# Turning all eight blocks of the gathered rows by DMA instead of four by DMA and four by TensorE

## The chip, the cores and the metric

The kernel runs on one core of a Trainium2 chip. The metric is the device time of one execution in microseconds (us); the time of a kernel is the median of its runs.

## The reference, cut to what matters

Four sequences of 512 tokens with 512 channels go through a gated attention-like layer and then a mixture-of-experts layer. The second one is where the change lies (2048 tokens, 8 experts with 352 hidden channels, two experts for each token):

```python
def _L0_ffn_ref(x, gate_w, gate_bias, shared_gw, shared_dw, up_w, down_w):
    xf = x.reshape(-1, C)
    yg = xf @ shared_gw.T
    y, g = jnp.split(yg, 2, axis=-1)
    shared = jax.nn.silu(g) * y @ shared_dw.T
    scores = jax.nn.sigmoid(xf @ gate_w.T)
    _, topk_idx = jax.lax.top_k(scores + gate_bias, 2)
    w = jnp.take_along_axis(scores, topk_idx, axis=-1)
    w = w / jnp.sum(w, axis=-1, keepdims=True)
    out = jnp.zeros_like(xf)
    for e in range(8):
        we = jnp.sum(jnp.where(topk_idx == e, w, 0.0), axis=-1)
        g_e, u_e = jnp.split(xf @ up_w[e].T, 2, axis=-1)
        out = out + (jax.nn.silu(g_e) * u_e) @ down_w[e].T * we[:, None]
    return (shared + out).reshape(B, T, C)
...
x = x + jnp.tanh(g_ffn[0]) * _L0_ffn_ref(_layernorm(x, axis=-1), ...)
```

## The kernel before, in words

**Before the experts.** The first 300 us hold the attention part, the shared expert and the router, batch by batch. The normalised rows of all tokens go to a table in HBM, `xn_rows`, in which each row is stored twice: 512 float16 numbers that are the rounded value (the high part), and 512 more that are what the rounding lost (the low part). The shared expert's result is stored to the output before the experts add to it.

**The expert tiles.** The router sorts the 4096 pairs of token and expert by expert into tiles of 128 rows, each tile of one expert; with the padding there are 39 (`SLOT_TILES`). For tile t:

- GpSimd gathers the tile's 128 rows, high and low part, 1024 columns, from `xn_rows` into one of four buffers (`gather`, line 562; `GATHERS` is 4). This is an indirect DMA, as are the adds below, and both go over one software queue.
- The rows must be turned so that the channels lie on the partitions, in blocks of 128 x 128: four blocks of the high part, four of the low. This is done in two ways. For tiles 0 to 7 (`BY_DMA` is 8) TensorE transposes all eight blocks into a bank of PSUM (`turn_gathered`, line 1053, and `turn_rows`, line 881, whose matmuls are on line 883), and VectorE copies them into the operand buffer `x_t` (`gathered_turned`, line 1608). For tiles 8 to 38 TensorE transposes the four high blocks alone and VectorE copies these; the four low blocks are turned by a DMA transpose that SyncE issues (`turn_low`, line 424) into one of four buffers `x_low`, two of which are halves of `x_t`.
- TensorE multiplies with the expert's up weights (`up`, line 1088; the matmuls of lines 1101 and 1102), ScalarE and VectorE form the hidden values, TensorE transposes them (line 1111) and multiplies with the down weights (`down`, line 1114; line 1121).
- ScalarE scales the result by the router's weight into one of two buffers `rows` (`expert_rows`, line 813; the activation is on line 816).
- GpSimd adds these 128 rows into the output in HBM by an indirect DMA that accumulates (`add_rows`, line 567; line 569). Two tiles can hold rows for the same token.

**What sets the order.** Everything is written out by hand, each engine its own list, with semaphores between them. TensorE's list in the expert tiles (`expert_steps`, line 1140) is: down of tile t, transposes of the gathered rows of tile t+3, the first half of up of tile t+2, the hidden transposes of tile t+1, the second half of up of tile t+2. From tile 8 on this is a loop of four tiles a turn; the tiles' experts are read from a table at its start. GpSimd's list is: gather tile t+4, wait until the add of tile t-1 has landed, add tile t:

```python
for t in range(SLOT_TILES):
    if t + GATHERS < SLOT_TILES:
        after(pool, xt_mm, TILES + t + 1)
        if t >= BY_DMA:
            after(pool, xl_ld[t % GATHERS], (t - BY_DMA) // GATHERS * 16 + 16)
        gather(t + GATHERS)
    if t:
        rows_added(t - 1)
    add_rows(t)
```

So a gather waits until the buffer's last tile has been turned, by TensorE (`xt_mm`) and by DMA (`xl_ld`). `rows_added` waits for the landing of an add and only then frees its buffer in `rows` (`rows_free`); ScalarE waits for that before it writes the buffer again, and TensorE's next down matmuls wait until ScalarE has emptied their bank (`y_sb`). SyncE's list in these tiles holds the DMA transposes alone, in the order of the tiles; each waits for its gather (`g_ld`) and for the up matmuls that last read its buffer (`up_mm`). The up matmuls wait for VectorE's copy (`xt_sb`) and, from tile 8 on, for the DMA transpose (`xl_ld`).

Of the kernel before, what the change touches and what calls it, by code (L numbers as in the profile page):

```python
# [3 lines left out]
BATCHES, SEQ, C, D = 4, 512, 512, 128  # L4
# [66 lines left out]
def build(nc, x, ctx_t, wq, wk, gates, gate_wt, gate_bias, weights, out, xn_rows):  # L71
# [12 lines left out]
    with ExitStack() as ctx:  # L84
# [44 lines left out]
        def work_buf(words):  # L129
            used[0] += words  # L130
            return work[:, used[0] - words:used[0]]
# [7 lines left out]
        x_low_more = work_buf(C).bitcast(F16).rearrange("p (s a c) -> p s a c", s=2, a=KC)  # L139
# [4 lines left out]
        x_low = [x_t[:, n, KC:, :] for n in range(2)] + [x_low_more[:, n, :, :] for n in range(2)]  # L144
# [27 lines left out]
        lg = sb("lg", [P, TILES, 2, EXPERTS])  # L172
        r = [m.rearrange("p (t e) -> p t e", t=TILES) for m in (wq_s, wk_s)]
        r += [sb(f"r{n}", [P, TILES, EXPERTS], F16 if n == 2 else F32) for n in range(2, 6)]
# [155 lines left out]
        def _(sp):  # L330
# [93 lines left out]
            def turn_low(t):  # L424
                after(sp, g_ld[t % GATHERS], (t // GATHERS + 1) * 16)
                after(sp, up_mm, Q0 + t - (2 if t < BY_DMA + 2 else GATHERS) + 1)
                sp.dma_start_transpose(out=x_low[t % GATHERS], in_=xg_slots[t % GATHERS][:, C:2 * C]).then_inc(xl_ld[t % GATHERS], 16)

            for t in range(BY_DMA, SLOT_TILES):
                turn_low(t)  # L430
# [4 lines left out]
        def _(pool):  # L435
# [149 lines left out]
            for t in range(SLOT_TILES):  # L585
                if t + GATHERS < SLOT_TILES:
                    after(pool, xt_mm, TILES + t + 1)
                    if t >= BY_DMA:
                        after(pool, xl_ld[t % GATHERS], (t - BY_DMA) // GATHERS * 16 + 16)
                    gather(t + GATHERS)  # L590
                if t:
                    rows_added(t - 1)
                add_rows(t)
# [246 lines left out]
        def _(pe):  # L840
# [40 lines left out]
            def turn_rows(src, bank_, blocks=2 * KC):  # L881
                for n in range(blocks):
                    mm = pe.transpose(bank_[:, n, :], src[:, n * P:(n + 1) * P], ident16[:])  # L883
                mm.then_inc(xt_mm, 1)
# [168 lines left out]
            def turn_gathered(t, slot, n, bank_=xt_ps, blocks=2 * KC):  # L1053
                pe.wait_ge(g_ld[slot], (n + 1) * 16)
                if bank_ is xt_ps:
                    after(pe, xt_sb, ROWS_DVE + t)
                turn_rows(xg_slots[slot], bank_, blocks)
# [30 lines left out]
            def up(t, p, item, ks, low=None, low_n=None):  # L1088

                if 0 in ks:  # L1090
                    after(pe, hid_sb, Q0 + t - 1)
                    after(pe, xt_sb, ROWS_DVE + t + 1)
                    if low is not None:
                        after(pe, xl_ld[low], low_n * 16)
                for k in ks:
                    at = k * 2 * H
                    for part in range(2):
                        lhs = x_low[p if low is None else low][:, k, :] if part else x_t[:, p, k, :]
                        for half in range(2 - part):
                            begin, end = (k, part, half) == (0, 0, 0), (k, part) == (KC - 1, 1)  # L1100
                            pe.matmul(pg[p][:, 0:H], lhs, w[:, item, half, at:at + H], start=begin, stop=end)  # L1101
                            mm = pe.matmul(pu[p][:, 0:H], lhs, w[:, item, half, at + H:at + 2 * H], start=begin, stop=end)  # L1102
                if KC - 1 in ks:
                    mm.then_inc(up_mm, 1)
# [23 lines left out]
            def turn_and_up(t, p, item, low=None, low_n=None):  # L1128
                up(t, p, ds(item, 1), range(0, KC // 2), low, low_n)
                turn_hidden(t - 1, 1 - p)  # L1130
                up(t, p, ds(item, 1), range(KC // 2, KC), low, low_n)
# [8 lines left out]
            def expert_steps(t0, n0, steps, turn=True, late=False, dma_from=0):  # L1140
                down_item = item_of(t0)
                for k in range(steps):
# [5 lines left out]
                    if turn:  # L1148
                        turn_gathered(t0 + k + 3, (k + 3) % GATHERS, n0 + (k + 3) // GATHERS,
                                      blocks=KC if k + 3 >= dma_from else 2 * KC)  # L1150
# [13 lines left out]
            expert_steps(t, t // GATHERS, 1, turn=False)  # L1164
# [7 lines left out]
        def _(dve):  # L1172
# [435 lines left out]
            def gathered_turned(t, p, uses, bank_=xt_ps, blocks=2 * KC):  # L1608
                after(dve, xt_mm, TILES + t + 1)
                after(dve, up_mm, Q0 + uses)  # L1610
                dve.tensor_copy(x_t[:, p, 0:blocks, :], bank_[:, 0:blocks, :]).then_inc(xt_sb, 1)
# [9 lines left out]
            def hidden_rows(t, p, turned=True):  # L1621
                hidden(t, p)
                hidden_low(t, p)
                if turned:
                    gathered_turned(t + 2, p, t + 1, blocks=KC)
                hidden_turned(t, p)

            for t in range(LATE_TILES):
# [4 lines left out]
                gathered_turned(t + 2, t % 2, t + 1, blocks=2 * KC if t + 2 < BY_DMA else KC)  # L1633
# [6 lines left out]
            for t in range(SLOT_TILES - 2, SLOT_TILES):  # L1640
                hidden_rows(t, t % 2, turned=False)
# [55 lines left out]
```

## Time and profile before

| | us |
|---|---|
| median of 3 runs | 544.96 (543.93 to 547.08) |
| the profiled execution | 546.4 |
| its span, first to last instruction | 544.6 |

| engine | busy us, share of the span |
|---|---|
| TensorE, matmuls (PE) | 491.2, 90% |
| TensorE, weight loads (PEld, beside the matmuls) | 271.8, 50% |
| VectorE (DVE) | 330.4, 61% |
| ScalarE (ACT) | 255.4, 47% |
| GpSimd (POOL) | 221.7, 41% |

The profile is of one execution; its times are counted from the start of the span. Shares of busy time are averages over stages that differ: the expert tiles take from about 300 us to the end. A DMA that SyncE issues shows in a timeline as an instruction of SyncE's queue (SPq), an indirect DMA as one of GpSimd; the duration shown is that of the issue, and the data moves after it. "Landing" is the time from the start of the issue to the last signal that the data has arrived; for the gathers and the DMA transposes the profile does not show it. The queues' shares are of the time of all 16 DMA engines of the core; queue q0 carries GpSimd's gathers and adds, q1 what SyncE issues.

### The profile page before, as it was taken

The page shows a single profiled execution, that of the slowest core. Times are in us where ns is not written, and L with a number is a line of the kernel's source. Part 1 is how long each engine was busy: PE and PEld are TensorE (multiplying, and loading weights), DVE is VectorE, ACT ScalarE, POOL GpSimd, SP SyncE. Part 2 cuts the span into 40 slices and gives each one's busy share as a digit, 9 for nine tenths or more (in the row PEclk, how much of TensorE's full clock was granted, in tenths as well). Part 3 has the DMA queues.
Part 4 walks back from the last instruction along what each step waited for, and adds up shares of the span by engine and source line. Part 5 has one row for each costly group of instructions (what it writes and reads, how often), then busy time and mean ns, then how long its engine had stood idle before and what let it go on. Part 6 is the DMA issues. An engine that isn't in the chain of part 4 may idle for free.

```text
span 544.6 us, 10400 instructions
## 1 busy us (share of the span) xinstructions
PE 491.2 (90%) x3021; PEld 271.8 (50%) x3022; DVE 330.4 (61%) x719; ACT 255.4 (47%) x465; POOL 221.7 (41%) x229
## 2 busy tenths in 40 slices
PE   7365998899979996899999999999999999999991
PEld 2233443444434444354655666665656665565650
DVE  1898799987888798779845774323333333323230
ACT  3683796776968496432312663222322222222220
POOL 2203268713984079401331444443334443344322
PEclk9669699999989998999999999999999999999997
DMA  6230332352443542140056897566565566656543
GB/s 212 113 103 21 120 101 70 97 177 89 132 112 99 187 108 77 72 166 2 0 149 233 231 259 132 98 110 112 101 111 97 106 102 113 112 97 108 98 55 39
DMA packets 45477, 61.57 MB, mean 113 GB/s; under 512 B 20544, under 2 KB 20800, under 8 KB 45440
## 3 DMA queue, kind: packets, MB, share of 16 engines
q1 hardware_dynamic: 36272, 40.53, 25.3%
q0 software_dynamic: 8736, 20.45, 21.7%
q8 instruction: 18, 0.29, 0.2%
q14 instruction: 19, 0.16, 0.1%
q10 hardware_dynamic: 432, 0.13, 0.1%
HBM read 37.90 MB, written 19.14 MB: 105 GB/s over the span
## 4 chain that ended last, share of the span: by engine, by line
PE 61%; DVE 20%; issue 5%; POOL 5%; ACT 5%; DMA 3%; DVEq 0%; POOLq 0%; ACTq 0%; SPq 0%
PE py L1121 14%; PE pg L1101 13%; PE pu L1102 12%; PE pg L949 5%; PE pu L949 5%; DVE w L1218 3%; DVE pa L1248 3%; PE pt_bank L883 3%; DVE w L1275 2%; PE pa L1111 2%; PE py L974 2%; DVE w L1252 2%; PE pa L1048 1%; DVE w L1198 1%; ACT w L666 1%
## 5 line engine op out<-in xcount | busy, mean ns | idle before, releaser
L1101 PE MATMUL pg<-w,x_t 128*128 x408 | 123.4, 313 | 0.3
L1102 PE MATMUL pu<-w,x_t 128*128 x408 | 123.3, 313 | 0.0
L569 POOL DMA_INDIRECT out<-rows,idx x39 | 61.8, 1585 | 136.7 <-ACT rows L816 125.7
L1121 PE MATMUL py<-w,work 128*128 x351 | 82.1, 379 | 0.8 <-DVE work L1606 0.8
L949 PE MATMUL pg<-w 128*128 128x512 f16 x288 | 77.3, 385 | 0.8 <-DVE work L1385 0.8
L806 ACT ACTIVATE work<-pg 128x352 f32<-128x352 f32 x39 | 18.1, 463 | 125.5 <-PE pu L1102 120.7
L949 PE MATMUL pu<-w 128*128 128x512 f16 x240 | 66.2, 385 | 0.0
L611 ACT ACTIVATE w<-stage 128x544 f16<-128x544 f32 x80 | 50.8, 648 | 31.5 <-DMA stage<-in_weights 31.0
L505 POOL TENSOR_TENSOR w<-stage,w 128x544 f16<-128x544 f32 x42 | 56.6, 1355 | 19.3 <-ACT stage L615 13.1
L1606 DVE COPY work<-pa 128x768 f16<-128x768 f16 x39 | 21.7, 557 | 62.3 <-PE pa L1111 57.9
L1595 DVE SCALAR_TENSOR_TENSOR work<-pu,work 128x352 f32<-128x352 f32 x39 | 20.5, 525 | 63.2 <-ACT work L806 59.6
L519 POOL TENSOR_TENSOR work<-work 128x512 f16<-128x512 f32 x20 | 26.4, 1318 | 71.9 <-ACT work L692 71.1
L1121 PEld LDWEIGHTS py<-w,work 128*128 128x128 f16 x351 | 34.3, 98 | 37.0 <-issue 0.9
L1101 PEld LDWEIGHTS pg<-w,x_t 128*128 128x128 f16 x408 | 39.9, 98 | 18.9 <-issue 2.1
L1102 PEld LDWEIGHTS pu<-w,x_t 128*128 128x128 f16 x408 | 39.9, 98 | 17.3 <-issue 0.2
L949 PEld LDWEIGHTS pg<-w 128*128 128x128 f16 x288 | 28.1, 99 | 34.9 <-issue 1.9
L949 PEld LDWEIGHTS pu<-w 128*128 128x128 f16 x240 | 23.8, 99 | 29.3 <-issue 1.7
L1218 DVE TENSOR_SCALAR_CACHE_REDUCE w<-w 128x512 f16<-128x512 f32 x48 | 33.9, 743 | 1.8 <-DVE w L1214 0.8
L816 ACT ACTIVATE rows<-py,w_slot 128x512 f32<-128x512 f32 x39 | 26.8, 687 | 14.0 <-PE py L1121 13.5
L1601 DVE TENSOR_TENSOR work<-work 128x352 f16<-128x352 f32 x39 | 20.4, 524 | 21.1 <-ACT work L811 21.1
L686 ACT ACTIVATE work<-pg 128x512 f32<-128x512 f32 (+1 forms) x24 | 14.1, 587 | 34.8 <-PE pu L949 33.3
L811 ACT ACTIVATE work<-work 128x352 f16<-128x352 f32 x39 | 19.3, 495 | 23.3 <-DVE work L1595 23.3
(235 smaller groups left out, 810.3 us busy)
## 6 DMA issues: line engine op xcount, KB each, us to landing
stage<-in_weights SPq DMA_DIRECT2D x80, 272.0 KB
xn_rows<-w SPq DMA_DIRECT2D x16, 256.0 KB, 2.6
out<-w SPq DMA_DIRECT2D x16, 256.0 KB, 2.8
w<-in_x SPq DMA_DIRECT2D x3, 1024.0 KB, 5.5
w<-in_ctx_t SPq DMA_DIRECT2D x4, 256.0 KB, 4.0
w<-in_x SPq DMA_DIRECT2D x2, 512.0 KB, 3.8
out<-rows,idx POOLq DMA_INDIRECT x39, 5.0
work<-xn_rows,idx POOLq DMA_INDIRECT x20
```

Source lines behind the costliest of these rows:

```text
L505: pool.tensor_tensor(w[:, ds(item, 1), 1, n * CHUNK_W:(n + 1) * CHUNK_W], stage[:, n % RING:n % RING + 1, :], w[:, ds(item, 1), 0, n * CHU ...
L519: pool.tensor_tensor(hid_tb[:, u, 1, :], hb[:, u % 2, :], hid_tb[:, u, 0, :], ALU.subtract).then_inc(hlo_sb, 1)
L569: pool.indirect_dma_start(out=out, out_offset=bass.IndirectOffsetOnAxis(ap=idx[:, t:t + 1], axis=0), in_=rows[:, t % 2, :], in_offset=None ...
L611: act.activation(w[:, ds(item, 1), 0, n * CHUNK_W:(n + 1) * CHUNK_W], stage[:, n % RING:n % RING + 1, :], ACT.Copy, scale=W_SCALE).then_in ...
L816: act.activation(rows[:, p, :], py[:, :], ACT.Copy, scale=w_slot[:, ds(t, 1)]).then_inc(y_sb, 1)
L949: mm = pe.matmul(bank_[:, :], w[:, half, part, at:at + P], x_tb[:, xpart * KC + k, :], start=(k, part, xpart) == (0, 0, 0), stop=(k, part) ...
L1101: pe.matmul(pg[p][:, 0:H], lhs, w[:, item, half, at:at + H], start=begin, stop=end)
L1102: mm = pe.matmul(pu[p][:, 0:H], lhs, w[:, item, half, at + H:at + 2 * H], start=begin, stop=end)
L1121: mm = pe.matmul(py[:, :], hid_t[:, p, part * JC + j, :], w[:, item, half, at:at + C], start=(j, part, half) == (0, 0, 0), stop=(j, part) ...
L1218: o.mark(dve.tensor_scalar(junk[:, i, :], sim[:, i, :], cur[:, i:i + 1], 0.0, ALU.is_ge, ALU.add, accum_out=counts[:, i:i + 1]))
L1595: dve.scalar_tensor_tensor(out=hid[:, p, :], in0=pu[p][:, 0:H], scalar=UP_UNSCALE * H_SCALE, in1=hid[:, p, :], op0=ALU.mult, op1=ALU.mult) ...
L1606: dve.tensor_copy(hid_t[:, p, :, :], hid_banks[p]).then_inc(ht_sb, 1)
```

## The change

From tile 8 on one DMA transpose turns all eight blocks of a tile, high and low part, 128 x 1024. It writes one of four operand buffers of eight blocks (`x_homes`) in place of the low blocks' buffers: the two of `x_t`, one that takes the place of `x_low_more` at twice the size, and one in memory that the router used before (`router`, in which `lg` and two of the router's other tiles now lie). TensorE's transposes of the high blocks and VectorE's copies of them are gone for tiles 8 to 38. GpSimd's gather waits from there on for the DMA transpose alone, the up matmuls as well. Tiles 0 to 7 are as before. The core of the diff:

```diff
--- before.py
+++ after.py
@@ -136,12 +136,13 @@
         hid16 = work_buf(2 * HP).bitcast(F16).rearrange("p (s a c) -> p s a c", s=2, a=2)
         hid_t = work_buf(2 * HP).bitcast(F16).rearrange("p (s a c) -> p s a c", s=2, a=2 * JC)
         hid = work_buf(2 * H).rearrange("p (a c) -> p a c", a=2)
-        x_low_more = work_buf(C).bitcast(F16).rearrange("p (s a c) -> p s a c", s=2, a=KC)
+        x_more = work_buf(C).bitcast(F16).rearrange("p (a c) -> p a c", a=2 * KC)
         assert used[0] <= UPS * SEQ
         xg = sb("xg", [P, 2, 2 * C], F16)
         xg_slots = [hb[:, n, :].bitcast(F16) for n in range(2)] + [xg[:, n, :] for n in range(2)]
         x_t = sb("x_t", [P, 2, 2 * KC, P], F16)
-        x_low = [x_t[:, n, KC:, :] for n in range(2)] + [x_low_more[:, n, :, :] for n in range(2)]
+        router = sb("router", [P, 2 * TILES * 2 * EXPERTS])
+        x_homes = [x_t[:, n, :, :] for n in range(2)] + [x_more, router[:, :].bitcast(F16).rearrange("p (a c) -> p a c", a=2 * KC)]
         rows = sb("rows", [P, 2, C])
         ident, ident16 = sb("ident", [P, P]), sb("ident16", [P, P], F16)
         scaled_ident, minus_ident = sb("scaled_ident", [P, P]), sb("minus_ident", [P, P], F16)
@@ -169,9 +170,10 @@
         spread = pt[:, 0, :]
         acc = sb("acc", [P, TPB // 2])
         missed, missed_i = sb("missed", [P, 1]), sb("missed_i", [1, 1], I32)
-        lg = sb("lg", [P, TILES, 2, EXPERTS])
+        lg = router[:, 0:TILES * 2 * EXPERTS].rearrange("p (t a e) -> p t a e", t=TILES, a=2)
         r = [m.rearrange("p (t e) -> p t e", t=TILES) for m in (wq_s, wk_s)]
-        r += [sb(f"r{n}", [P, TILES, EXPERTS], F16 if n == 2 else F32) for n in range(2, 6)]
+        r += [sb(f"r{n}", [P, TILES, EXPERTS], F16 if n == 2 else F32) for n in range(2, 4)]
+        r += [router[:, n * TILES * EXPERTS:(n + 1) * TILES * EXPERTS].rearrange("p (t e) -> p t e", t=TILES) for n in (2, 3)]
 
         rc = sb("rc", [P, 7, TILES])
         re8 = sb("re8", [P, 6, EXPERTS])
@@ -421,13 +423,13 @@
             for s in sh_st:
                 after(sp, s, TILES // 2 * 16)
 
-            def turn_low(t):
+            def turn_gathered(t):
                 after(sp, g_ld[t % GATHERS], (t // GATHERS + 1) * 16)
                 after(sp, up_mm, Q0 + t - (2 if t < BY_DMA + 2 else GATHERS) + 1)
-                sp.dma_start_transpose(out=x_low[t % GATHERS], in_=xg_slots[t % GATHERS][:, C:2 * C]).then_inc(xl_ld[t % GATHERS], 16)
+                sp.dma_start_transpose(out=x_homes[t % GATHERS], in_=xg_slots[t % GATHERS]).then_inc(xl_ld[t % GATHERS], 16)
 
             for t in range(BY_DMA, SLOT_TILES):
-                turn_low(t)
+                turn_gathered(t)
             after(sp, rows_free, SLOT_TILES)
 
 
@@ -584,8 +586,9 @@
                 after(pool, s, TILES // 2 * 16)
             for t in range(SLOT_TILES):
                 if t + GATHERS < SLOT_TILES:
-                    after(pool, xt_mm, TILES + t + 1)
-                    if t >= BY_DMA:
+                    if t < BY_DMA:
+                        after(pool, xt_mm, TILES + t + 1)
+                    else:
                         after(pool, xl_ld[t % GATHERS], (t - BY_DMA) // GATHERS * 16 + 16)
                     gather(t + GATHERS)
                 if t:
@@ -878,8 +881,8 @@
                         mm = pe.transpose(turn_banks[i][:, j * P:(j + 1) * P], kept[:, j, i * P:(i + 1) * P], ident[:])
                     mm.then_inc(at_mm, 1)
 
-            def turn_rows(src, bank_, blocks=2 * KC):
-                for n in range(blocks):
+            def turn_rows(src, bank_):
+                for n in range(2 * KC):
                     mm = pe.transpose(bank_[:, n, :], src[:, n * P:(n + 1) * P], ident16[:])
                 mm.then_inc(xt_mm, 1)
 
@@ -1050,11 +1053,11 @@
                               start=(step, n) == (0, 0), stop=(step, n) == (SLOTS_STEPS - 1, SLOTS_STEP - 1),
                               skip_group_check=True).then_inc(hot_mm, 1)
 
-            def turn_gathered(t, slot, n, bank_=xt_ps, blocks=2 * KC):
+            def turn_gathered(t, slot, n, bank_=xt_ps):
                 pe.wait_ge(g_ld[slot], (n + 1) * 16)
                 if bank_ is xt_ps:
                     after(pe, xt_sb, ROWS_DVE + t)
-                turn_rows(xg_slots[slot], bank_, blocks)
+                turn_rows(xg_slots[slot], bank_)
 
             logits(BATCHES - 1)
             for u in range(UPS):
@@ -1085,17 +1088,18 @@
 
             weights_ready(LATE)
 
-            def up(t, p, item, ks, low=None, low_n=None):
+            def up(t, p, item, ks, home=None, home_n=None):
 
                 if 0 in ks:
                     after(pe, hid_sb, Q0 + t - 1)
-                    after(pe, xt_sb, ROWS_DVE + t + 1)
-                    if low is not None:
-                        after(pe, xl_ld[low], low_n * 16)
+                    if home is None:
+                        after(pe, xt_sb, ROWS_DVE + t + 1)
+                    else:
+                        after(pe, xl_ld[home], home_n * 16)
                 for k in ks:
                     at = k * 2 * H
                     for part in range(2):
-                        lhs = x_low[p if low is None else low][:, k, :] if part else x_t[:, p, k, :]
+                        lhs = x_homes[p if home is None else home][:, part * KC + k, :]
                         for half in range(2 - part):
                             begin, end = (k, part, half) == (0, 0, 0), (k, part) == (KC - 1, 1)
                             pe.matmul(pg[p][:, 0:H], lhs, w[:, item, half, at:at + H], start=begin, stop=end)
@@ -1125,10 +1129,10 @@
             def item_of(t):
                 return pe.value_load(tile_e[0:1, ds(t, 1)], min_val=HALVES, max_val=ITEMS - 1)
 
-            def turn_and_up(t, p, item, low=None, low_n=None):
-                up(t, p, ds(item, 1), range(0, KC // 2), low, low_n)
+            def turn_and_up(t, p, item, home=None, home_n=None):
+                up(t, p, ds(item, 1), range(0, KC // 2), home, home_n)
                 turn_hidden(t - 1, 1 - p)
-                up(t, p, ds(item, 1), range(KC // 2, KC), low, low_n)
+                up(t, p, ds(item, 1), range(KC // 2, KC), home, home_n)
 
             pe.wait_ge(table_ok, 1)
             after(pe, y_sb, TILES - 1)
@@ -1137,7 +1141,7 @@
             turn_gathered(2, 2, 0)
             turn_and_up(1, 1, item_of(1))
 
-            def expert_steps(t0, n0, steps, turn=True, late=False, dma_from=0):
+            def expert_steps(t0, n0, steps, late=False, dma_from=0):
                 down_item = item_of(t0)
                 for k in range(steps):
                     if k:
@@ -1145,9 +1149,8 @@
                     down(t0 + k, k % 2, ds(down_item, 1))
                     if k == 0:
                         next_item, up_item = item_of(t0 + 1), item_of(t0 + 2)
-                    if turn:
-                        turn_gathered(t0 + k + 3, (k + 3) % GATHERS, n0 + (k + 3) // GATHERS,
-                                      blocks=KC if k + 3 >= dma_from else 2 * KC)
+                    if k + 3 < dma_from:
+                        turn_gathered(t0 + k + 3, (k + 3) % GATHERS, n0 + (k + 3) // GATHERS)
                     if late and LATE <= t0 + k + 2 + HALVES < ITEMS:
                         weights_ready(t0 + k + 2 + HALVES + 1)
                     turn_and_up(t0 + k + 2, k % 2, up_item, *(((k + 2) % GATHERS, n0 + (k + 2) // GATHERS - BY_DMA // GATHERS + 1)
@@ -1161,7 +1164,7 @@
             with pe.Fori(2, loops) as i:
                 expert_steps(i * GATHERS, i, GATHERS)
             t = SLOT_TILES - 3
-            expert_steps(t, t // GATHERS, 1, turn=False)
+            expert_steps(t, t // GATHERS, 1)
             t = SLOT_TILES - 2
             down(t, t % 2, ds(item_of(t), 1))
             turn_hidden(t + 1, (t + 1) % 2)
@@ -1605,10 +1608,10 @@
                 after(dve, down_mm, TILES + t - 1)
                 dve.tensor_copy(hid_t[:, p, :, :], hid_banks[p]).then_inc(ht_sb, 1)
 
-            def gathered_turned(t, p, uses, bank_=xt_ps, blocks=2 * KC):
+            def gathered_turned(t, p, uses, bank_=xt_ps):
                 after(dve, xt_mm, TILES + t + 1)
                 after(dve, up_mm, Q0 + uses)
-                dve.tensor_copy(x_t[:, p, 0:blocks, :], bank_[:, 0:blocks, :]).then_inc(xt_sb, 1)
+                dve.tensor_copy(x_homes[p], bank_).then_inc(xt_sb, 1)
 
 
             gathered_turned(0, 0, 0)
@@ -1618,11 +1621,9 @@
             gathered_turned(1, 1, 0, xt_second)
             shared_rows(BATCHES - 1, TPB - 1)
 
-            def hidden_rows(t, p, turned=True):
+            def hidden_rows(t, p):
                 hidden(t, p)
                 hidden_low(t, p)
-                if turned:
-                    gathered_turned(t + 2, p, t + 1, blocks=KC)
                 hidden_turned(t, p)
 
             for t in range(LATE_TILES):
@@ -1630,7 +1631,8 @@
                 for piece in late_pieces(t)[:PER_TILE // 2]:
                     low_piece(*piece)
                 hidden_low(t, t % 2)
-                gathered_turned(t + 2, t % 2, t + 1, blocks=2 * KC if t + 2 < BY_DMA else KC)
+                if t + 2 < BY_DMA:
+                    gathered_turned(t + 2, t % 2, t + 1)
                 hidden_turned(t, t % 2)
                 for piece in late_pieces(t)[PER_TILE // 2:]:
                     low_piece(*piece)
@@ -1638,7 +1640,7 @@
                 for k in range(2):
                     hidden_rows(i * 2 + k + 1, 1 - k)
             for t in range(SLOT_TILES - 2, SLOT_TILES):
-                hidden_rows(t, t % 2, turned=False)
+                hidden_rows(t, t % 2)
 
 
 def kernel(x, ctx_512, g_xattn, g_ffn, L0_xattn_Wq, L0_xattn_Wk, L0_xattn_gamma_raw, L0_ffn_gate_w, L0_ffn_gate_bias,
```

## Rows read from the trace of the kernel before

**Rows 1.** The page, part 4: the chain that ended last, by engine.

```profile
PE 61%; DVE 20%; issue 5%; POOL 5%; ACT 5%; DMA 3%; DVEq 0%; POOLq 0%; ACTq 0%; SPq 0%
```

**Rows 2.** Chain of waits in order of time: start, duration (us), engine, tile, line.

```profile
305.06 1.94 PE py L1121 x9
307.00 0.45 PE pt_bank L883 x8
...
311.37 1.94 PE py L1121 x9
...
398.36 1.94 PE py L1121 x9
...
417.28 1.94 PE py L1121 x9
...
423.36 1.94 PE py L1121 x9
...
437.82 0.22 PE pt_bank L883 x4
```

**Rows 3.** The same chain at the end of the span.

```profile
532.29 4.70 DMA out<-rows,idx
...
537.87 1.55 POOL out L569
```

**Rows 4.** Timeline of ScalarE: start, duration, operation, idle time before and its releaser.

```profile
534.60 0.69 ACT L816 ACTIVATE rows<-py,w_slot 128x512 f32<-128x512 f32 x1 [3.11 <-PE py L1121]
```

**Rows 5.** Timeline of GpSimd, its adds and one gather, columns alike.

```profile
340.03 1.59 POOL L569 DMA_INDIRECT out<-rows,idx  x1 [3.37 <-ACT rows L816]
...
420.88 1.59 POOL L569 DMA_INDIRECT out<-rows,idx  x1 [2.84 <-ACT rows L816]
422.77 0.98 POOL L564 DMA_INDIRECT work<-xn_rows,idx  x1 [0.30 <-issue]
427.08 1.59 POOL L569 DMA_INDIRECT out<-rows,idx  x1 [3.33 <-ACT rows L816]
...
520.34 1.57 POOL L569 DMA_INDIRECT out<-rows,idx  x1 [4.46 <-ACT rows L816]
```

**Rows 6.** Landings of adds, median us: 343:520; 519:540; at 420.88 and 427.08; at 476.52.

```profile
out<-rows,idx POOLq DMA_INDIRECT x28, 5.1
...
out<-rows,idx POOLq DMA_INDIRECT x4, 4.7
...
out<-rows,idx POOLq DMA_INDIRECT x1, 5.3
...
out<-rows,idx POOLq DMA_INDIRECT x1, 5.2
```

**Rows 7.** VectorE's copies of turned rows, 343 to 522: count, busy, mean, idle before.

```profile
L1611 DVE COPY x_t<-pt_bank 128x512 f16<-128x512 f16 x29 | 12.2, 419 | 1.8 <-PE pt_bank L883 1.7
```

**Rows 8.** One stretch: length, busy us of PE, PEld, DVE, ACT, POOL; PEclk, DMA share, GB/s.

```profile
343.00:522.00 179.00, 177.44 (x1241) 108.79 (x1240) 56.97 (x116) 47.32 (x87) 72.68 (x56) 1.00 0.60 104
```

**Rows 9.** Timeline of SyncE's queue, the DMA transpose of tile 24.

```profile
427.63 1.19 SPq L427 DMA_TRANSPOSE x_t<-work  x1
```

**Rows 10.** DMA queues (packets, MB, share): 400:500; 428.7:429.5; 429.5:431.9; 478.5:478.8; 478.8:481 (two); slices of 532.3:537.

```profile
q1 hardware_dynamic: 8704, 2.10, 10.9%
...
q1 hardware_dynamic: 503, 0.13, 77.9%
...
q0 software_dynamic: 157, 0.32, 100.0%
...
q1 hardware_dynamic: 127, 0.03, 52.5%
...
q0 software_dynamic: 139, 0.27, 80.7%
q1 hardware_dynamic: 323, 0.08, 25.6%
...
DMA  0000000000000000059497399448999983210000
```

## The prediction

> **What bounds the kernel now.** I read the page first, then the chain of waits in order of time, the timelines of ScalarE and GpSimd, and last the DMA queues in windows of about a microsecond. The chain that ended last is TensorE's for 61% of the span [rows 1]; in the expert tiles it shows no wait for data. In order of time it repeats one figure per tile: nine down matmuls (1.94 us), the transposes of a gathered row tile, then up matmuls. With eight transposes (tiles before 8) that piece takes 0.45 us and the tile 6.31 us (305.06 to 311.37); with four, 0.22 us and 6.08 us (417.28 to 423.36). One tile in four holds idle time at the edge of the loop as well, so that four tiles take 25.0 us (398.36 to 423.36), 6.25 each [rows 2].
>
> So far this is a TensorE bound. But look at the end of the chain: the last add into the output starts at 537.87, for it waits for the add before, which took 4.70 us from issue to landing; 0.88 us more passed until the next was issued [rows 3]. ScalarE had the last rows ready at 535.3 [rows 4]. The adds are a serial chain of their own: each is issued after the last has landed. From 340.03 to 520.34 there are 29 steps of it, 6.22 us each [rows 5], and the median landing in that stretch is 5.1 us [rows 6]. Landing plus 0.9 us is 6.0: this second chain runs only 0.2 us a tile behind the first. Where an add lands late it sets the pace already: one issued at 420.88 lands after 5.3 us, at 426.2, and the next comes at 427.08, the same 0.9 us later [rows 5, 6].
>
> **The change, part by part.**
> *TensorE's four transposes go*, for tiles 8 to 38: 31 tiles x 0.22 us = 6.8 us, all on TensorE's path [rows 2]. The idle time at the loop's edge follows the down matmuls; it stays and then stands before the up matmuls. TensorE alone would need 6.22 - 0.22 = 6.00 us a tile.
>
> *VectorE's copies go*: 29 of 419 ns in that stretch [rows 7]. VectorE is busy 57 of 179 us there [rows 8], and nothing but the removed operand waited for the copy. Zero; the cover is its idle two thirds.
>
> *Waits.* The up matmuls no longer wait for the copy, only for the DMA transpose, as they already do for the low parts. Tile 24 is gathered at 422.77, right behind the add of tile 19 [rows 5], and its transpose is issued at 427.63 [rows 9]; its up matmuls start only after 437.8 [rows 2], ten microseconds later. Issue and data of a doubled transpose (3 to 5 us, below) fit. GpSimd's gather loses its wait for TensorE and keeps the one for the transpose of four tiles earlier, landed long before: zero. On SyncE nothing but these transposes is queued, one each 6.2 us with 1.19 us of issue [rows 9]; even 2.4 us fits: zero. The fourth operand buffer lies in memory that the router has done with: zero.
>
> *DMA work doubles.* A transpose of four blocks is 512 packets of 256 bytes; 503 of them filled 78% of the 16 engines' time in a window of 0.8 us, 428.7 to 429.5 [rows 10]. Eight blocks should take about 0.75 us longer. As load that is little: the engines are busy 0.60 of the stretch [rows 8], of which the transposes' queue holds 0.11 [rows 10]; that becomes about 0.71.
>
> *What stands behind it on the engines* is the add. The gather goes out just behind an add, lands after it, and its landing releases the transpose when the next add is being issued: 427.63 against 427.08 [rows 5, 9]. An add's packets follow its issue by 2.0 us where nothing is in the way (532.29, first packets in slice 18 of 40, at 534.3). From 427.08 that would be 429.1; but up to 429.5 only the transposes' queue has packets, and behind it the adds' queue fills the engines [rows 10]. That add landed after 5.3 us, like its neighbour; without transposes, at the end of the span, the median is 4.7 [rows 6]. So the transposes of today cost the adds about 0.4 us. Yet at 478.5, when a transpose had only just begun as an add came, both queues have packets from 478.8 on, the adds 81% and the transposes 26% of the time [rows 10]; that add landed after 5.2 us [rows 6].
>
> The trace shows no transpose of eight blocks. Bounds for what 0.75 us more of it adds to each landing: from below nothing (today's packets in front, the rest alternating with the add, as at 478.8); a gain I exclude, since nothing is taken from this queue. From above all 0.75 us (the add held to the end, as at 429.5). Neither row is nearer, for an add will find part of the packets queued and part still to come: I take half, 0.37 us. The landing is then 5.1 + 0.37 = 5.47 us and a step 5.47 + 0.9 = 6.37, longer than TensorE's 6.00: **the adds become the bound**. What TensorE saves turns into a wait of the down matmuls: they need ScalarE to empty their bank, and ScalarE needs a free rows buffer, which an add gives back when it lands.
>
> **Sum.** 29 steps x (6.37 - 6.22) = +4.4 us. Behind them the last three steps, 520.34 to 537.87, are 17.5 us today [rows 3, 5]; bound by the adds at 5.6 each (4.7 + 0.9) they are 16.8: -0.7. Together +3.7 us. The profiled execution took 546.4 us (544.6 of span and 1.8 around it), so 550.1 against its own time; it lies 1.4 above the median of the runs, 544.96, and on that I forecast 548.7. [...]
>
> [...]
>
> **Rivals.**
> *The adds aren't held longer, and TensorE's gain arrives.* Packets alternate, or the longer transpose begins behind the add. For it speak the windows from 478.8 on, where an add went ahead among a transpose's packets [rows 10]; against it the held add of 427.08. The step is 5.1 + 0.9 = 6.0, like TensorE's; 29 x 0.22 = 6.4 us less, and 0.4 to 0.7 behind: 538.2, or 541 if landings grow by 0.1. [...]
>
> *The adds are held to the transposes' end.* For it the window up to 429.5 and the landings of 5.3 us; against it the alternation at 478.8. Landing 5.85, step 6.75, 29 x 0.53 = 15.4, less 0.7: +14.7, 559.7. Of all that can turn the change into a loss this is the one mechanism; it decides from about 0.25 us of extra holding, where the step passes 6.22.
>
> *Both cancel.* The extra holding is 0.2 to 0.25 us, the steps stay near 6.2 and the time at 544 to 546: off one chain, onto its twin.
>
> That the change does not do what it says would be seen at once: matmuls of line 883 behind tile 7, or transposes that still have some 512 packets.
>
> **How the numbers follow.** A measurement of this kernel can tell about 0.5% (2.7 us) from no change. The forecast, with its own range of 545.5 to 553, gets 0.42, of which 0.10 lies within 0.5%. The first rival, 537.5 to 541, gets 0.31, all faster: one of the two kinds of window speaks for it. Holding to the end, 556 to 563: 0.12, slower. Cancelling: 0.15, of which 0.14 within and 0.01 faster. That makes faster 0.32, the same 0.24, slower 0.44. The range goes from 538 to 557; it leaves out most of the full holding and a little at the bottom.
>
> **What would show it.** Right: GpSimd's adds 6.3 to 6.4 us apart, each issued 0.9 us after the landing of the one before; landings of 5.4 to 5.5 us; a chain of waits that runs through the output's DMA from tile 8 on; idle time of TensorE ahead of the down matmuls; over 1,000 packets per transpose, spread over some 1.5 us. Wrong: landings that stay at 5.1 us, with the chain still on TensorE at 6.0 us a tile. An issue on SyncE of over 5 us, or up matmuls that wait for a transpose, would make it another mechanism altogether.

## The result and the profile after

The changed kernel takes 554.33 us (median of 4 runs, 551.83 to 556.74) against 545.54 us for the kernel before on the same chip: a ratio of 1.0161, with a 95% interval from 1.0104 to 1.0218. That is 8.8 us slower. The forecast was slower by 3.7 us. The time lies in the whole range given, 538 to 557, though not in the 545.5 to 553 that the forecast claimed for itself.

The spans of the two profiled executions are 551.6 and 544.6 us. First the page of the changed kernel, part 4, then its chain of waits in order of time (start, duration, what), to be laid beside [rows 1] and [rows 2]:

```profile
DMA 40%; PE 20%; DVE 17%; ACT 9%; issue 8%; POOL 4%; POOLq 0%; ACTq 0%; DVEq 0%; SPq 0%
...
305.63 5.85 DMA out<-rows,idx
...
423.39 5.60 DMA out<-rows,idx
...
429.21 0.70 ACT rows L819
...
429.91 5.73 DMA out<-rows,idx
...
435.81 0.70 ACT rows L819
...
436.56 5.52 DMA out<-rows,idx
```

Where the chain went through TensorE's matmuls, it now goes from one add into the output to the next. GpSimd's timeline of the same kernel (start, duration, operation, idle time before and its releaser) gives the steps, against [rows 5]; below it the landings of the adds issued from 343 to 520, against [rows 6], and the stretch 343 to 522, with busy us of PE, PEld, DVE, ACT and POOL, granted clock, DMA share and GB/s, against [rows 8]:

```profile
339.63 1.59 POOL L571 DMA_INDIRECT out<-rows,idx  x1 [4.77 <-DMA out<-rows,idx]
...
423.39 1.59 POOL L571 DMA_INDIRECT out<-rows,idx  x1 [3.32 <-ACT rows L819]
...
429.91 1.59 POOL L571 DMA_INDIRECT out<-rows,idx  x1 [3.64 <-ACT rows L819]
...
528.21 1.57 POOL L571 DMA_INDIRECT out<-rows,idx  x1 [5.19 <-ACT rows L819]
...
out<-rows,idx POOLq DMA_INDIRECT x27, 5.7
...
343.00:522.00 179.00, 168.59 (x1109) 100.63 (x1107) 45.03 (x84) 46.14 (x84) 70.29 (x55) 1.00 0.68 122
```

From 339.63 to 528.21 there are the same 29 steps as in the kernel before: 6.50 us each, where they were 6.22, and 8.3 us more in all. Every step is one landing and 0.9 us; the one issued at 423.39 lands at 428.99, and the next comes at 429.91. The last three steps, from 528.21 to 545.00, take 16.8 us in place of 17.5. So of the span's 7.0 us these are 8.3, less 0.7, less 0.4 by which the first of these adds was earlier. TensorE was busy for 177.4 of the 179 us before; now it is idle for 10.4 of them, with the granted clock still at 1.00.

ScalarE's lines in the chain mislead. The profile puts an add down to the last signal before it, and that is ScalarE's; but the rows that ScalarE writes at 429.21 are those of the next tile, and it had waited for the same landing. The rows of the add of 429.91 were ready at 423.3. ScalarE's timeline shows both:

```profile
422.63 0.69 ACT L819 ACTIVATE rows<-py,w_slot 128x512 f32<-128x512 f32 x1 [1.25 <-POOLq L576]
...
429.21 0.69 ACT L819 ACTIVATE rows<-py,w_slot 128x512 f32<-128x512 f32 x1 [1.06 <-POOLq L576]
```

One thing in these spans is hardly the change's. The first add of all came at 299.24, 3.0 us earlier than in the kernel before (302.27), and 2.6 of these were lost by 339.63, in six steps of 6.7 us in place of 6.3. The adds issued at 305.63, 312.40 and 319.19 landed late, after 5.9 to 6.0 us, before any DMA transpose had begun. In the runs below those six steps take 6.3 to 6.4 us each, so this belongs to the one execution; its cause is open.

What holds an add is seen in the queues around the one issued at 429.91. Its transpose is issued at 430.31 (SyncE's timeline). The DMA queues in two windows, 431.4 to 432.85 and 432.85 to 435.3 (packets, MB, share of the 16 engines):

```profile
430.31 1.23 SPq L429 DMA_TRANSPOSE x_t<-work  x1
...
q1 hardware_dynamic: 1022, 0.26, 92.7%
q0 software_dynamic: 5, 0.01, 10.9%
...
q0 software_dynamic: 173, 0.39, 101.8%
q1 hardware_dynamic: 34, 0.00, 2.0%
```

For 1.45 us hardly anything but the transpose moves, then hardly anything but the adds' queue, the add first and a gather behind it. The first packet of an add came 2.1 to 2.2 us after its issue where nothing was ahead of it (all 30 adds from 343 to 520 in the run with the transposes behind the add, below); here it was due at 432.0 or 432.1 and came at 432.8. The window is that of 428.7 to 429.5 in [rows 10] at nearly twice the length. The packets in the two traces show that it is no exception: of the 27 adds issued from 343 to 520 in the changed kernel every one begins when a transpose's packets run out, 2.4 to 3.0 us after its issue (median 2.8). In 22 of them at most 31 of the transpose's 1024 packets are then left, in the other five 87 to 183. In the kernel before, the first packets came 2.2 to 2.5 us after the issue (median 2.3). The packets of a transpose of eight blocks took 1.41 us (median from 343 to 520), where those of four blocks took 0.76 in the kernel before.

### The profile page after: what moved, and what is told of

The parts are those of the page before. It is cut to its first block, busy times and chain, and to the rows that moved or that the text cites. A ratio compares the mean times of both kernels' runs of the same rounds, so it can differ in the third digit from the quotient of the medians.

```text
span 551.6 us, 9974 instructions
## 1 busy us (share of the span) xinstructions
PE 485.5 (88%) x2897; PEld 266.6 (48%) x2898; DVE 318.9 (58%) x688; ACT 255.6 (46%) x465; POOL 221.5 (40%) x229
## 4 chain that ended last, share of the span: by engine, by line
DMA 40%; PE 20%; DVE 17%; ACT 9%; issue 8%; POOL 4%; POOLq 0%; ACTq 0%; DVEq 0%; SPq 0%
DMA out<-rows,idx 37%; PE pg L952 5%; PE pu L952 5%; ACT rows L819 3%; DVE w L1221 3%; DVE w L1278 2%; DVE pa L1251 2%; PE py L977 2%; DMA stage<-in_weights 2%; PE pa L1051 1%; ACT w L669 1%; ACT w L614 1%; DVE w L1327 1%; PE pu L977 1%; DVE w L1255 1%
## 5 line engine op out<-in xcount | busy, mean ns | idle before, releaser
L1105 PE MATMUL pg<-w,x_t 128*128 x288 | 86.7, 313 | 5.6 <-DMA x_t<-work 5.6
L1106 PE MATMUL pu<-w,x_t 128*128 x288 | 86.6, 313 | 0.0
L1105 PEld LDWEIGHTS pg<-w,x_t 128*128 128x128 f16 x288 | 28.1, 98 | 22.5 <-issue 9.7
L1106 PEld LDWEIGHTS pu<-w,x_t 128*128 128x128 f16 x288 | 28.1, 98 | 13.5
L1105 PE MATMUL pg<-w,work 128*128 x96 | 28.9, 313 | 4.2 <-DMA work<-xg 2.1
```

## The experiments

Two theories stood against each other from here: that the adds are held by what SyncE queues ahead of them, and that the up matmuls now wait for the transposes. For the second speaks a view of TensorE's waits in the changed kernel from 340 to 525 (who waited for what: us in total, times, longest); below it a gather on GpSimd's timeline and one of these waits on TensorE's:

```profile
PE pg L1105 <- DMA x_t<-work: 5.6, 8, 1.4
PE pg L1105 <- DMA router<-xg: 2.7, 3, 1.3
PE pg L1105 <- issue: 2.0, 4, 0.6
PE pg L1105 <- DMA work<-xg: 1.3, 1, 1.3
...
425.28 0.99 POOL L566 DMA_INDIRECT work<-xn_rows,idx  x1 [0.30 <-issue]
...
435.06 0.32 PE L1105 MATMUL pg<-w,x_t 128*128 x1 [0.24 <-DMA x_t<-work]
```

The waits for the transposes are 9.6 us, about the size of the loss. No down matmul is in this list. The first four experiments start from the kernels as they are, with one thing moved. Of each edit the lines that matter are shown.

**TensorE's transposes put back.** GpSimd's gather waits for them again too.

```diff
+                    elif turn:
+                        turn_gathered(t0 + k + 3, (k + 3) % GATHERS, n0 + (k + 3) // GATHERS, blocks=KC)
```

> The changed kernel with TensorE's four transposes of the high blocks put back for tiles 8 to 38; their result is used by nobody, the DMA transposes still turn all eight blocks. Theory (the adds into the output are a serial chain, and the longer DMA transposes hold each of them): TensorE has idle time under that chain, so the 6.8 us of transposes cost nothing: 552 to 556 us, steps between adds 6.5 us as in the changed kernel. Rival (TensorE still sets the pace in most tiles and the loss lies elsewhere, for example in the weight loads of tiles 0 to 6): the work comes back on the path, 559 to 563 us.

Measured: 555.59 us, ratio to the kernel before 1.0193 (1.0141 to 1.0245), beside 1.0161 for the change alone: the intervals overlap. The landings stay at 5.7 us ("x27, 5.7" in the same view as above), and the 27 steps from 350.36 to 527.00 are 6.54 us each. The 6.8 us of TensorE work cost nothing that could be measured in the changed kernel: they lie in the idle time under the adds.

**Four blocks by DMA in place of eight.** The up matmuls read these four for both parts.

```diff
-                sp.dma_start_transpose(out=x_homes[t % GATHERS], in_=xg_slots[t % GATHERS]).then_inc(xl_ld[t % GATHERS], 16)
+                sp.dma_start_transpose(out=x_homes[t % GATHERS][:, 0:KC, :], in_=xg_slots[t % GATHERS][:, 0:C]).then_inc(xl_ld[t % GATHERS], 16)
```

> The changed kernel with DMA transposes of four blocks in place of eight (the high blocks alone, and the up matmuls read them for both parts; so the low parts are left out of the computation). Theory: transposes run 0.75 us as before, adds land after 5.0 to 5.2 us, steps are 6.0 to 6.1 us, and a part of TensorE's gain arrives: 537 to 542 us. Rival (the second chain of adds has no part in it, and TensorE's time is what counts): the full 6.8 us, 537.5 to 539 us, with TensorE busy without a gap. If the loss has nothing to do with the length of the transposes: 552 to 556 us.

Measured: 541.79 us, ratio 0.9911 (0.9876 to 0.9946). Its landings from 343 to 520, and two adds 28 steps apart:

```profile
out<-rows,idx POOLq DMA_INDIRECT x30, 5.1
...
347.86 1.59 POOL L571 DMA_INDIRECT out<-rows,idx  x1 [2.73 <-ACT rows L819]
...
518.70 1.57 POOL L571 DMA_INDIRECT out<-rows,idx  x1 [4.67 <-DMA out<-rows,idx]
```

Landings as in the kernel before, steps of 6.10 us. So the doubled transpose is what turns a gain into a loss; and even without it only about 4 of TensorE's 6.8 us would arrive, since a landing of 5.1 and 0.9 us make 6.0.

**The transposes behind the add.** One more wait of SyncE: the add of four tiles earlier has landed.

```diff
                 after(sp, up_mm, Q0 + t - (2 if t < BY_DMA + 2 else GATHERS) + 1)
+                after(sp, rows_free, t - GATHERS + 1)
```

> The changed kernel, each DMA transpose from tile 8 on held until the add that it stands in the way of has landed (SyncE waits for the add of four tiles earlier). Same work, same DMA bytes, transposes issued some 5 us later. Theory (the add is held behind a transpose that starts just before it): the transposes now run between two adds, first packets of an add 2.2 us after its issue in place of 2.8, landings 4.7 to 5.0 us, TensorE sets the pace at 6.0 us a tile: 537 to 542 us. Rival 1 (the up matmuls wait for the transposes, of which the trace shows 9.6 us): later transposes make it worse, 565 us and more. Rival 2 (it is the load of the DMA engines, 0.68 in place of 0.60): no difference, 552 to 556 us.

Measured: 539.84 us, ratio 0.9897 (0.9852 to 0.9942); in a second group 540.38 us, 0.9889 (0.9852 to 0.9927). Same work, same bytes, 14 us less than the changed kernel, and less than the kernel before. The page's part 4; the landings; the stretch 343 to 522; one transpose and the add behind it; and the queues in 416.0 to 417.5 (first line) and 417.75 to 420.3:

```profile
PE 61%; DVE 18%; ACT 7%; issue 6%; POOL 4%; DMA 3%; DVEq 0%; POOLq 0%; ACTq 0%; SPq 0%
...
out<-rows,idx POOLq DMA_INDIRECT x30, 4.8
...
343.00:522.00 179.00, 175.32 (x1161) 105.56 (x1158) 47.72 (x89) 48.63 (x89) 74.25 (x57) 1.00 0.69 126
...
414.86 1.23 SPq L430 DMA_TRANSPOSE work<-xg  x1
...
415.68 1.59 POOL L572 DMA_INDIRECT out<-rows,idx  x1 [2.90 <-ACT rows L820]
...
q1 hardware_dynamic: 1056, 0.26, 91.6%
...
q0 software_dynamic: 178, 0.40, 98.6%
```

The transpose is issued 0.8 us before the add, not 0.4 after it, and is over when the add's packets are due (415.68 + 2.1 = 417.8). None of the 30 adds issued from 343 to 520 finds a transpose in front: all begin 2.1 to 2.2 us after their issue. The chain is TensorE's again. The DMA share is no lower than in the changed kernel (0.69 and 0.68), so the load is not the cause; and transposes that come later made nothing worse, so the 9.6 us of TensorE's waits were a consequence. In this run TensorE waits for no transpose from 343 to 522. In the changed kernel it had run ahead to the tile that was just being gathered: the gather goes out behind an add (425.28 behind 423.39), the transpose follows it (430.31), and the up matmuls that wait for it start at 435.06. Both rivals fall here.

**The same wait in the kernel before.** The diff is the line above.

> The kernel before with the same added wait of SyncE: transposes of four blocks, held until the add of four tiles earlier has landed. Theory: landings fall from 5.1 to 4.7 to 4.9 us, but TensorE sets the pace there with its 6.2 us a tile, so next to nothing comes of it: 541 to 546 us. Rival 1 (waits of the up matmuls for the transposes count): slower, over 548 us.

Measured: 545.33 us, ratio 0.9991 (0.9957 to 1.0025). The landings fall from 5.1 to 4.8 us and bring nothing: as long as TensorE needs 6.2 us a tile, the adds have just enough room. The wait is worth something only together with the change.

**Half of each add.** In both kernels `idx[0:P // 2, t:t + 1]` and `rows[0:P // 2, t % 2, :]` in `add_rows`.

> The changed kernel with adds of 64 of each tile's 128 rows (half of the adds is left out). Theory (the chain of adds is the bound): an add moves half the data, lands after 4.3 to 4.8 us even behind a transpose, the step falls under TensorE's 6.0 us, and TensorE's gain shows: 534 to 541 us, TensorE without waits but those for the loop's edge. Rival (the transposes themselves, by the waits of the up matmuls or the load of the engines, set the pace): 548 us or more.

> The kernel before with adds of 64 of each tile's 128 rows. Theory: TensorE sets the pace there at 6.2 us a tile, so only the last adds after TensorE's end get shorter, 1 to 3 us: 541 to 545 us. If the adds were the bound before the change too: under 540 us.

Measured: the changed kernel 533.87 us, ratio 0.9790 (0.9728 to 0.9852); the kernel before 540.27 us, 0.9883 (0.9822 to 0.9944). With adds that land after 3.8 and 3.6 us neither kernel is bound by them, and the change then gains 6.4 us, nearly the 6.8 worked out for TensorE. The kernel before came out a little below what was expected, and just above the 540 us under which its adds would have been called a bound before the change too. In its stretch TensorE has no idle time left, where [rows 8] has 1.6 us of it:

```profile
343.00:522.00 179.00, 178.97 (x1260) 111.16 (x1259) 56.91 (x117) 48.34 (x89) 69.03 (x57) 1.00 0.43 85
```

So the idle time at the edges of TensorE's loop goes when the adds get shorter; how the two are tied, these runs do not show.

**The transposes put off by about 2 us.**

```diff
+                sp.dma_start(warm[0:1, :], one1[0:1, :]).then_inc(aside, 16)
+                sp.wait_ge(aside, (t - BY_DMA + 1) * 16)
                 sp.dma_start_transpose(out=x_homes[t % GATHERS], in_=xg_slots[t % GATHERS]).then_inc(xl_ld[t % GATHERS], 16)
```

> The changed kernel, each DMA transpose put off by one tiny copy that SyncE waits for, some 2 us, so that its data starts when the add is already moving. Theory (what is queued first goes first; an add under way is only shared with): first packets of an add 2.2 us after its issue, landings 5.0 to 5.4 us, steps 6.0 to 6.3 us, 538 to 548 us. Rival (a transpose of 1.4 us costs an add that much wherever it meets it): 552 us and more, landings 5.6 us.

Measured: 543.32 us, ratio 0.9954 (0.9920 to 0.9988), landings 4.9 us. Each transpose was issued 2.4 us after its copy (median of 31; 1.5 to 3.5). The time is the one expected, but the trace does not show the meeting that the edit was made for. One transpose and the add behind it; then the queues in 424.7 to 426.6 (first line) and 427.1 to 428.9:

```profile
423.51 1.25 SPq L432 DMA_TRANSPOSE router<-xg  x1
...
425.10 1.59 POOL L574 DMA_INDIRECT out<-rows,idx  x1 [3.47 <-DMA out<-rows,idx]
...
q1 hardware_dynamic: 1055, 0.26, 95.0%
...
q0 software_dynamic: 107, 0.22, 100.2%
```

The transpose is not late for an add but ahead of the next one, and over before that one's packets come. Of the 29 adds issued from 343 to 520 only 3 find a transpose in front. Ten transposes begin while an add is moving, near its end, and 120 to 293 of their 1024 packets fall within it; those adds' last packets end no later than the others' (4.1 to 4.8 us after the issue, against 4.2 to 5.1). So this run shows once more, by other means than the wait, that adds landed early (4.9 us in the median) where no transpose was ahead of them (26 of the 29). What a transpose costs that meets an add just after its start, it does not show.

**Twelve blocks a tile.**

```diff
+                after(sp, aside, (t - BY_DMA) * 16)
+                sp.dma_start_transpose(out=nowhere, in_=xg_slots[t % GATHERS][:, 0:C]).then_inc(aside, 16)
                 sp.dma_start_transpose(out=x_homes[t % GATHERS], in_=xg_slots[t % GATHERS]).then_inc(xl_ld[t % GATHERS], 16)
```

> The changed kernel with a further DMA transpose of four blocks ahead of each tile's, into a buffer that nobody reads: twelve blocks a tile, 0.75 us more data. Theory (an add is held until the last packet of the transposes ahead of it): steps 7.1 to 7.3 us in place of 6.5, 29 times 0.6 to 0.75 us: 570 to 577 us. Rival (an add is held by a first part only, the rest alternates with it): landings grow by 0.2 us or less, 553 to 561 us.

Measured: 541.97 us, ratio 0.9924 (0.9886 to 0.9962): more DMA work than the changed kernel and 12 us less. Both expectations missed. The stretch 343 to 522; the add issued at 425.04, with the two transposes after it; and the queues in 426.6 to 427.5 (two lines) and 427.5 to 429.9 (two lines):

```profile
343.00:522.00 179.00, 171.59 (x1134) 103.33 (x1133) 46.81 (x88) 47.88 (x88) 73.11 (x56) 1.00 0.87 148
...
425.04 1.59 POOL L576 DMA_INDIRECT out<-rows,idx  x1 [3.56 <-DMA work<-xg]
...
425.55 1.19 SPq L432 DMA_TRANSPOSE work<-work  x1
426.79 1.49 SPq L433 DMA_TRANSPOSE x_t<-work  x1
...
q1 hardware_dynamic: 512, 0.13, 70.2%
q0 software_dynamic: 2, 0.00, 5.3%
...
q0 software_dynamic: 142, 0.26, 81.6%
q1 hardware_dynamic: 450, 0.11, 26.3%
```

The extra transpose of four blocks, issued first, holds this add as in the kernel before. The one of eight is issued 1.24 us later, and by the time its packets come the add is under way: the two take turns, and that add lands after 5.2 us. It is not the rule: of the 29 adds issued from 343 to 520 nine are held like this, with first packets 2.3 to 2.6 us after the issue; the other 20 begin after 2.1 to 2.2, with no transpose in front. In these runs an add was held by what was queued ahead of it when its packets were due, not by the sum of what SyncE issued: landings of 5.0 us with twelve blocks a tile, of 5.7 us with eight. From this came the next one.

**Two DMAs of four blocks.**

```diff
+                for part in range(2):
+                    sp.dma_start_transpose(out=x_homes[t % GATHERS][:, part * KC:(part + 1) * KC, :],
+                                           in_=xg_slots[t % GATHERS][:, part * C:(part + 1) * C]).then_inc(xl_ld[t % GATHERS], 16)
```

> The changed kernel with each tile's eight blocks turned by two DMA transposes of four, the high part's first, one issued right after the other. Same blocks, same bytes, same waits. Theory, as the twelve blocks left it (a DMA that is queued ahead of the add holds it to its end; one issued while the add is being queued or moved takes turns with it): only the first 0.75 us stands ahead of the add, landings 4.9 to 5.2 us, steps about 6.0, 538 to 544 us. Rival (the eight blocks hold the add by their whole length, 1.4 us, and the twelve were fast for another reason): 551 to 556 us.

Measured: 547.73 us, ratio 1.0030 (1.0002 to 1.0058), landings 5.3 us. The same blocks and bytes in two DMAs rather than one: 6.6 us less than the changed kernel, though 4 us over what was expected, for landings did not go back to 5.1. So cutting the transpose in two helps, though less than expected. Why this is 1% slower than the twelve blocks, which do more, the packets show in part: here 22 of the 28 adds issued from 343 to 520 find a transpose in front (first packets 2.3 to 2.6 us after the issue), there 9 of 29, with landings of 5.0 us. What places the transposes so differently in the two runs stays open.

**TensorE's loop written out**, on top of the transposes behind the add: `for i in range(2, loops)` in place of the loop of the engine.

> The same kernel (transposes behind the add) with TensorE's loop of four tiles written out. In its trace a tile takes 5.86 us between down matmuls, but 6.5 to 6.7 at each of seven loop edges; the first two rounds of four tiles, which are written out before the change too, show no such edge. If the edge is the loop's, 7 times 0.65 us go: 4 to 5 us less, 534 to 536 us, where the adds (4.8 us and 0.9) still fit under 5.86. If it is the reading of the tiles' experts from the table: no difference.

Measured: 536.99 us, ratio 0.9838 (0.9799 to 0.9876), 3.4 us less than the same kernel with its loop in the same group (540.38). The gaps at the loop's edges, 0.5 to 0.6 us before the up matmuls at the seven edges from 343 to 522 of the first run with the loop, are gone from the trace: they were the loop's. This is the fastest kernel here that does the whole computation; its adds land after 4.9 us and bind again in part (DMA has 17% of its chain, where the kernel with the loop had 3 or 4%).

## Why the prediction was right

*The chain of adds.* Read off the last two adds, it was taken as a second chain 0.2 us a tile behind TensorE. It became the bound: steps of one landing and 0.9 us, and the output's DMA in the chain of waits. In the profiled execution that begins with the add of 305.63, tile 1, by the late landings told above; with TensorE's transposes put back it begins at tile 7, about where it was forecast. The halved adds show it from the other side: where they are short, TensorE's gain is there, 6.4 us.

*TensorE's 6.8 us.* The term was right and not on the path any more; putting the work back cost nothing that could be measured.

*The hold.* This is the mis-sized term. The prediction took half of 0.75 us, 0.37, between a row for holding and one for taking turns. Of the median landing it measured 5.7 - 5.1 = 0.6 us, and the mean step is 6.50 in place of 6.37. Both factors were off, in opposite ways. A transpose queued ahead held the add to its end, or nearly (in 22 of 27 adds at most 31 of its 1024 packets were left), and not by half; and eight blocks took 0.65 us longer than four (1.41 and 0.76), not 0.75. The row for holding was the nearer one. The row for taking turns, at 478.5, showed a transpose that had started too late to be ahead: its first packets came some 0.1 us before the add's were due. (The 2.0 us of lead that the prediction read off a row of slices are 2.1 to 2.2 by the packets; no term of its sum hangs on it.)

*The sum.* 29 steps of +0.15 us were forecast, +0.28 came, 8.3 us in place of 4.4; the last three steps were forecast at 16.8 us and took 16.8. In the medians of the times that is +8.8 against +3.7. The sign, the place and the new bound were right, the size was less than half. That the time still lies in the range is owed to its width: it lies nearer to the 556 at which the rival of full holding began than to 548.7.

*TensorE's wait.* What TensorE saves was to turn into a wait of the down matmuls, for a rows buffer. This step was wrong: from 340 to 525 no down matmul waits. The up matmuls do, which were given ten microseconds of slack on the transposes: 12 times, 9.6 us in all. The slack was read in a kernel in which TensorE was the bound; where TensorE runs ahead of the adds, it comes up to the next gather, which goes out only behind an add, and the slack is used up. It cost nothing, but the prediction said that such waits would point to another mechanism, and that was wrong too. Of the other zeros, SyncE's issue took 1.23 us, not 2.4; leaving VectorE's copies out was not tried by itself. The granted clock was 1.00 in the stretch 343 to 522 of both kernels, with TensorE idle for 1.6 us of it before and for 10.4 after.

*The rivals.* "Not held longer" was ruled out by the steps, and by the four blocks at 541.8 as the price of the difference. "Held to the end" was right about the holding; with its 0.75 us in every landing it came out 5 us above the result. What happened is its mechanism at a smaller size, rather than the half holding of the forecast.

## What to carry to other kernels

When one engine is the bound, look for the second chain behind it before moving work off it: here landing plus issue of a serial chain of accumulating DMAs was 0.2 us a tile short of the bound, and that is all the room the change had. A transfer off the path can have a price all the same: the transposes, queued just ahead of the adds, took their landings to 5.7 us, where they were 4.8 with nothing ahead, and moving them out of the way, with a single wait, turned 1.6% of loss into 1.0% of gain. The busy share of the DMA engines said little about this: 0.87 with two transposes a tile (541.97 us) was faster than 0.68 with one (554.33 us).

## What the runs showed of the hardware that was not expected

A DMA transpose of eight blocks kept SyncE for 1.23 us (median in the changed kernel), one of four for 1.19 (in the kernel before): the issue hardly grew with the size (it took 1.49 us right behind another one, in the run with twelve blocks). A DMA transpose queued ahead of an accumulating DMA held it until its packets ran out: with eight blocks the add's first packets came 0.6 us late in the median of 27 adds (2.8 us after the issue in place of 2.2), while a DMA issued 1.2 us later took turns with it (one add, at 425.04 with twelve blocks a tile). An edge of TensorE's loop of four tiles cost 0.5 to 0.6 us (seven edges with the transposes behind the add); with the adds halved TensorE's idle time there was gone from the kernel before (busy for 178.97 of 179 us), and with the loop written out the changed kernel got 3.4 us faster. What ties the edge to the DMA traffic was not tried.
